# Long-convolution block on one core: the second convolution's windows loaded into 32 partitions, the taps in eight copies

## The reference, cut to what matters

```
q, k, v = u @ Wq.T + bq, u @ Wk.T + bk, u @ Wv.T + bv      # as [batch, channel, position]
k  = causal_conv(k, k_kernel) + k_D * k                    # first convolution, 512 taps a channel
y  = causal_conv(k * v, ssm_kernel) + D * (k * v)          # second convolution, 512 taps a channel
x  = layernorm(u + (y * q) @ Wo.T + bo)
x  = layernorm(x + spikes(relu(x @ W_fc.T)**2 @ W_proj.T))
```

## Time and profile before

| What | Value |
|---|---|
| Median of 3 runs | 1033.93 us (1029.09 to 1037.75) |
| Profiled execution, its own time | 1030.6 us |
| Its span, from the first instruction to the last | 1028.6 us |
| TensorE matmuls busy | 791.5 us, 77% |
| VectorE busy | 712.0 us, 69% |
| ScalarE busy | 521.7 us, 51% |
| Granted TensorE clock over the span | 0.894 |
| Main loop (first to last start of L976) | 78.7 to 479.9 us |

### The profile page before, as it was taken

One profiled execution on the slowest core, in us unless ns is written; L12 is line 12 of the kernel. 1 busy time (PEld: TensorE's weight loads), 2 busy tenths in 40 slices (PEclk: granted clock), 3 DMA queues, 4 the chain that ended last, 5 costly groups with the idle time before them and its releaser, 6 DMA issues.

```text
span 1028.6 us, 27885 instructions
## 1 busy us (share of the span) xinstructions
PE 791.5 (77%) x12032; PEld 648.2 (63%) x12032; DVE 712.0 (69%) x1087; ACT 521.7 (51%) x560; POOL 385.7 (37%) x306
## 2 busy tenths in 40 slices
PE   0186878787768888845499888898888998889983
PEld 0186878787767787845356566665566665666652
DVE  6983555555536665747559877888777878778884
ACT  3475646574645565431445544555445555455551
POOL 0261211121101112200455446655456544565542
PEclk9998989898888989976589998999899989989997
DMA  9898898888767788897000111100111101111001
GB/s 347 287 300 225 181 237 181 227 182 222 177 135 164 157 184 179 184 209 206 20 1 1 42 41 41 41 18 22 41 41 41 36 5 41 41 41 39 2 21 41
DMA packets 39292, 118.35 MB, mean 115 GB/s; under 512 B 3872, under 2 KB 23200, under 8 KB 31008
## 3 DMA queue, kind: packets, MB, share of 16 engines
q1 hardware_dynamic: 37824, 114.71, 43.3%
q10 hardware_dynamic: 1376, 2.23, 0.6%
HBM read 106.69 MB, written 27.01 MB: 130 GB/s over the span
## 4 chain that ended last, share of the span: by engine, by line
issue 25%; DMA 20%; POOL 19%; PE 18%; DVE 14%; ACT 3%; POOLq 0%; SPq 0%; DVEq 0%; ACTq 0%
DMA arena<-kpad_dram 18%; POOL arena L596 10%; PE ps L670 10%; PE ps L648 4%; POOL arena L603 2%; DVE arena L1048 2%; DVE arena L956 2%; POOL arena L585 2%; PE ps L764 2%; DVE arena L1067 2%; POOL arena L590 2%; DVE arena L939 2%; POOL arena L600 1%; PE ps L771 1%; PE ps L728 1%
## 5 line engine op out<-in xcount | busy, mean ns | idle before, releaser
L670 PE MATMUL ps<-arena 128*128 128x64 f16 (+3 forms) x6144 | 190.7, 187 | 78.6 <-DVE arena L956 41.8
L596 POOL TENSOR_TENSOR arena<-arena 128x512 f16<-128x512 f32 x128 | 165.8, 1314 | 198.0 <-ACT arena L484 194.3
L670 PEld LDWEIGHTS ps<-arena 128*128 128x128 f16 x6144 | 185.8, 101 | 81.9 <-issue 80.6
L432 ACT ACTIVATE arena<-arena 64x3584 f16<-64x3584 f16 x60 | 188.7, 3182 | 51.4 <-DVE arena L939 51.3
L648 PE MATMUL ps<-arena 128*128 128x96 f16 x3072 | 150.6, 214 | 74.4 <-DVE arena L901 51.2
L771 PE MATMUL ps<-arena 128*128 128x256 f16 x1536 | 192.7, 287 | 8.7 <-POOL arena L596 6.1
L648 PEld LDWEIGHTS ps<-arena 128*128 128x128 f16 x3072 | 144.9, 103 | 77.1 <-issue 71.1
L771 PEld LDWEIGHTS ps<-arena 128*128 128x128 f16 x1536 | 157.3, 104 | 42.1 <-POOL arena L596 10.8
L764 PE MATMUL ps<-arena 128*128 128x512 f16 x768 | 170.5, 382 | 2.5 <-DVE arena L1074 2.5
L939 DVE TENSOR_TENSOR arena<-arena 64x512 f16<-64x512 f16 x128 | 67.1, 533 | 151.3 <-DMA arena<-kpad_dram 151.2
L555 POOL TENSOR_TENSOR arena<-arena 128x512 f16<-128x512 f32 x32 | 42.7, 1337 | 278.5 <-ACT arena L426 278.5
(11 more groups left out here) (91 smaller groups left out, 702.2 us busy)
## 6 DMA issues: line engine op xcount, KB each, us to landing
arena<-kpad_dram SPq DMA_DIRECT2D x128, 512.0 KB, 6.9
kpad_dram<-ksplit_dram SPq DMA_DIRECT2D x16, 1024.0 KB, 12.1
qy<-in_uT SPq DMA_DIRECT2D x8, 1024.0 KB, 17.5
arena<-in_u SPq DMA_DIRECT2D x16, 512.0 KB, 4.1
out<-arena SPq DMA_DIRECT2D x16, 512.0 KB, 3.0
arena<-in_k SPq DMA_DIRECT2D x2, 512.0 KB, 4.8
ksplit_dram<-arena ACTq DMA_DIRECT2D x2, 512.0 KB, 3.8
arena<-in_wfT SPq DMA_DIRECT2D x1, 1024.0 KB, 13.8
```

Of the source, the lines that this page charges most:

```text
L432: nc.scalar.activation(*shifted(windows_of(0, s, half)), ACT.Copy).then_inc(c1_copied, 1)
L596: nc.gpsimd.tensor_tensor(h16[:, 1, f], h_square[:, f % 4], h16[:, 0, f], ALU.subtract).then_inc(h_lo, 1)
L670: last = nc.tensor.matmul(out[:, ch * COL + delta * B:(ch + 1) * COL], win[:, delta * P:(delta + 1) * P], data(xp, ch)[:, 0:cols], start=( ...
```

## The change

`kpad_dram` holds 8 copies in place of 16. The spreads are made for each group of eight channels in place of each chunk of 32: 64 DMAs with rows of 1 KB (SLICE // 16 = 512 elements) and 8 copies, in place of 16 DMAs with rows of 4 KB and 16 copies. Three groups are spread before the first window load, five more behind the first six window loads, and then one group in each step, eight ahead. The window load of each group waits for its own group's spread.

The second convolution's windows are loaded into partitions 0 to 31 in place of 0 to 63. VectorE masks 32 columns in 32 partitions, copies partitions 0 to 31 to 32 to 63, 32 columns to the right (`shifted_quarter`), and then copies 0 to 63 to 64 to 127 as before. Both widening copies come ahead of both old copies. The first convolution's windows are still loaded into 64 partitions.

```diff
-NCOPY = 16
-SLICE = CH * 2 * L
-EARLY = 4
+NCOPY = 8
+SLICE = G * 2 * L
+AHEAD = 8
+NKP = 2 * AHEAD
...
+        def shifted_quarter(windows):
+            t = windows.rearrange("p c a n -> p (c a) n")
+            return t[QP:HP, :, QP:L], t[0:QP, :, 0:L - QP]
...
-                at, n = piece * SLICE, SLICE // NCOPY
+                at, n = g * SLICE, SLICE // 16
-                    sp.dma_start(dst, src.unsqueeze(1).to_broadcast([NCOPY, NCOPY, n])).then_inc(kpad_out[piece], 16)
+                    sp.dma_start(dst, src.unsqueeze(1).to_broadcast([16, NCOPY, n])).then_inc(kpad_out[g % NKP], 16)
...
-                sp.dma_start(windows[0:HP].rearrange("p c a n -> p (c a n)"),
-                             bass.AP(first.tensor, first.offset, [[ROWS - HP // NCOPY, NCOPY], [-1, HP // NCOPY], [1, row]])
+                parts = QP if conv else HP
+                sp.dma_start(windows[0:parts].rearrange("p c a n -> p (c a n)"),
+                             bass.AP(first.tensor, first.offset,
+                                     [[ROWS - parts // NCOPY, NCOPY], [-1, parts // NCOPY], [1, row]])
                              ).then_inc(t_in[slot], 16)
...
-            spread(0)
+            for g in range(3):
+                spread(g)
             sp.wait_ge(kpad_head, 16)
-            sp.wait_ge(kpad_out[0], 32)
...
-            for piece in range(1, EARLY):
-                spread(piece)
+            for g in range(3, AHEAD):
+                spread(g)
...
-                if s % GPC == 0 and s // GPC + EARLY < NC:
-                    spread(s // GPC + EARLY)
+                if s + AHEAD < NG:
+                    spread(s + AHEAD)
...
                 for half in range(2):
                     dve.wait_ge(c2_masked, 2 * g + half + 1)
+                    nc.vector.tensor_copy(*shifted_quarter(windows_of(1, s, half, final(g)))).then_inc(c2_widened, 1)
+                for half in range(2):
+                    dve.wait_ge(c2_widened, 2 * g + half + 1)
                     nc.vector.tensor_copy(*shifted(windows_of(1, s, half, final(g)))).then_inc(c2_copied, 1)
```

More of the change, by code:

```diff
@@ L27 @@
 HP = P // 2
+QP = P // 4
 ROWS = P + D * 2 * L
-NCOPY = 16
-SLICE = CH * 2 * L
-EARLY = 4
+NCOPY = 8
+SLICE = G * 2 * L
+AHEAD = 8
+NKP = 2 * AHEAD
 NU = 8
@@ L198, in build @@
             sem(n) for n in ("kpad_zero", "kpad_hi", "kpad_lo", "kpad_head", "ksplit_out", "w16_out"))
-        kpad_out = [sem(f"kpad_out{n}") for n in range(NC)]
+        kpad_out = [sem(f"kpad_out{n}") for n in range(NKP)]
         t_in = [sem(f"t_in{n}") for n in range(8)]
@@ L204, in build @@
             sem(n) for n in ("t_zero", "c1_masked", "c2_masked", "c1_copied", "c2_copied"))
-        c1_copied_dve, c1_half, c2_half = (sem(n) for n in ("c1_copied_dve", "c1_half", "c2_half"))
+        c1_copied_dve, c1_half, c2_half, c2_widened = (
+            sem(n) for n in ("c1_copied_dve", "c1_half", "c2_half", "c2_widened"))
         ld_wcur = [sem(f"ld_wcur{r}") for r in range(2)]
@@ L283, in _, with spread @@
                              uT.rearrange("(t p) n -> p t n", p=P)[:, :, n * UP:(n + 1) * UP]).then_inc(ld_u[n], 16)
-            def spread(piece):
-                at, n = piece * SLICE, SLICE // NCOPY
+            def spread(g):
+                at, n = g * SLICE, SLICE // 16
                 for conv in range(2):
@@ L296, in load_windows @@
                 first = kpad_dram[conv, 0, P + (2 * g + half) * row:]
-                if g % GPC == 0 and conv == 0 and half == 0:
-                    sp.wait_ge(kpad_out[g // GPC], 32)
+                if conv == 0 and half == 0:
+                    sp.wait_ge(kpad_out[g % NKP], 32 * (g // NKP + 1))
                 second_place = conv == 1 and g >= NG - GPC and g % 2 == 0
@@ L839, in _ @@
             nc.vector.memset(T[HP:P].rearrange("p k c a n -> p (k c a) n")[:, :, 0:HP], 0.0).then_inc(t_zero, 1)
+            nc.vector.memset(T[QP:HP, 4:6].rearrange("p k c a n -> p (k c a) n")[:, :, 0:QP], 0.0).then_inc(t_zero, 1)
             link(nc.vector.memset(part_max[:, :], 0.0))
@@ L937, in mask @@
                     dve.wait_ge(t_in[4 + half], 16 * (g + 1))
-                tri = windows_of(conv, s, half, final(g))[0:HP].rearrange("p c a n -> p (c a) n")[:, :, 0:HP]
-                nc.vector.tensor_tensor(tri, tri, causal[0:HP, 0:HP].unsqueeze(1).to_broadcast([HP, 2 * HG, HP]),
+                n = QP if conv else HP
+                tri = windows_of(conv, s, half, final(g))[0:n].rearrange("p c a n -> p (c a) n")[:, :, 0:n]
+                nc.vector.tensor_tensor(tri, tri, causal[0:n, 0:n].unsqueeze(1).to_broadcast([n, 2 * HG, n]),
                                         ALU.mult).then_inc((c1_masked, c2_masked)[conv], 1)
@@ L955, in windows2 @@
                     dve.wait_ge(c2_masked, 2 * g + half + 1)
+                    nc.vector.tensor_copy(*shifted_quarter(windows_of(1, s, half, final(g)))).then_inc(c2_widened, 1)
+                for half in range(2):
+                    dve.wait_ge(c2_widened, 2 * g + half + 1)
                     nc.vector.tensor_copy(*shifted(windows_of(1, s, half, final(g)))).then_inc(c2_copied, 1)
             dve.wait_ge(id_done, 2)
-            dve.wait_ge(t_zero, 1)
+            dve.wait_ge(t_zero, 2)
             for quarter in range(GPC):
@@ L1009, in _ @@
                                      ).then_inc(t_zero, 1)
-                    dve.wait_ge(t_zero, 2)
+                    nc.vector.memset(T2[QP:HP].rearrange("p k c a n -> p (k c a) n")[:, :, 0:QP], 0.0
+                                     ).then_inc(t_zero, 1)
+                    dve.wait_ge(t_zero, 4)
                 if s == PAIR - 2:
```

## The result

| | Kernel before | Changed kernel |
|---|---|---|
| Median | 1034.65 us (1029.09 to 1037.75, 4 runs) | 1059.1 us (1053.16 to 1062.83, 4 runs) |
| Ratio to before | | 1.0237, 95% interval 1.0168 to 1.0306 |
| Profiled execution | 1030.6 us, span 1028.6 | 1062.83 us, span 1061.1 |
| Main loop, first to last start of `times_v` | 401.2 us | 434.8 us |

The change makes the kernel slower by 24.5 us. The profiled executions lie 32 us apart, because the one of before is quicker than its median and the one of after slower; what follows reads places and kinds of waits from the traces, and sizes from medians.

A forecast was written before the change was run, and what follows sets the result against it. A loop through late window loads, VectorE's copies and conv2 was taken to bound the kernel. Main-loop steps of 14.0 us (29) and 17.5 (two) gave 441 us for 401, +40, so 1074 us; range 1008 to 1100.

The forecast's parts named there:

- Eight engines for window loads: Main loop: window loads on eight engines instead of keeping their rate take the forecast from 1012 to 1074 us.
- Eight copies put the loads on eight engines: Window loads: the source pattern's outermost count, now eight, cuts each transfer into eight shares on eight engines.
- A first-convolution load takes 4.8 us: Main loop: transfer into 64 partitions at 13.7 GB/s for each of eight engines, between bounds of 2.4 and 4.8 us.
- rival 1: Window loads keep 220 GB/s on 16 or eight engines; step stays 11.1 us, total 1012; chance 0.27 together with Rival 4.
- The widening costs 2.2 us behind the last landing: VectorE in the main loop: two widening copies of 1.16 us each delay conv2 by some 2.2 us every step.
- The half loads pay exactly for it: Main loop: at unchanged load rate, shorter second-convolution loads offset the widening, leaving the step at 11.1 us.
- The equation T = (6.0 + 2.4 + transfers + tail) / 2: Main-loop step: 6.0 us to the first load's issue, 2.4 fixed, transfers, work behind last landing; 11.1 before, 13.5 after.
- The bursts cost 20.3 us: Main loop before: the four steps behind spread bursts cost 20.3 us more than plain ones; the change removes this.
- Stalls of TensorE would be half hidden: Main loop: TensorE's stalls cost 0.9 us a step; about half is hidden by 2.4 us more slack, giving 14.0.
- Rival 2: Main loop: engines drift apart, a load takes about 3.2 us; -4 us, about 1030, no difference; chance 0.13.
- Rival 3: Main loop: instruction fetches share the eight full engines, 1 to 1.5 us more a step, about 1109; within the 0.60 case.
- Rival 4: Main loop: VectorE's 9.9 us of work becomes the limit, adding 0.3 us a step, 1020; chance 0.27 together with rival 1.

The follow-up runs named there:

- e3: Kernel before with only the spreads changed to eight channels each step; 16 copies, all loads into 64 partitions, no widening: 1022.04 us, ratio 0.9897.
- e1: Changed kernel with 16 copies in place of eight, all else of the change kept: 1005.5 us, ratio 0.972.
- e9: e1 with its 16 stored copies, but the window loads' source pattern names only eight of them: 1059.82 us, ratio 1.0217.
- e10: e1 with its 16 stored copies, but the window loads' source pattern names only four of them: 1167.8 us, ratio 1.1261.
- e4: Kernel before with eight copies in place of 16 as the only change, all window loads into 64 partitions: 1122.45 us, ratio 1.0853.
- e2: Changed kernel, eight copies, with each first-convolution load into 64 partitions issued as two loads of 32: 1013.59 us, ratio 0.9809.
- e5: e3 with the two widening copies added, rewriting what the loads had already put there: 1052.72 us, ratio 1.0144.
- e6: e1 without the two widening copies, leaving a quarter of each second-convolution tile out of the computation: 983.53 us, ratio 0.9495.

## Why the prediction was right, point by point

The forecast was slower, 1074 us, with 1050 to 1108 for its case; 1059.1 is in it, by the mechanism that it named. The size is less good: 24.5 us in place of 40. By medians the change comes apart like this:

| Term | Forecast | Measured | From |
|---|---|---|---|
| Fine spreads in place of bursts | -22 (1012 - 1034) | -12.8 | e3 against before |
| Half loads and widening together | 0 | -16.5 | e1 against e3 |
| Eight engines for window loads | +62 (1074 - 1012) | +53.6 | changed kernel against e1 |
| Sum | +40 | +24.3 | |

The second and third terms came out 16.5 and 8.4 us below the forecast, the first 9.2 above. That the total lies only 15.7 us off is partly luck.

*Eight copies put the loads on eight engines.* Right. e9 shows that the outermost count of the pattern does it, as the Trainium skill has it (DMA: Bandwidth & Descriptors, "Why a DMA increments its semaphore by 16 and not by 1"); a window load's semaphore has eight raises at its end in the changed kernel, four in e10 and 16 in e1, and the DMA shares of 0.47 in the changed kernel and 0.51 in e4 are eight of 16 engines.

*A first-convolution load takes 4.8 us.* Nearly right: 4.5, by the landings. It is no constant, since e4's loads of the same shape took 3.9 with the engines full. A half load took 1.2 where the forecast had 1.3. The reason that was given, engines crowding into a part of the partitions, fits e2 and not e10, and stays unproven. With other rows for each engine (e2) the time comes within 8 us of sixteen engines, which is rival 1 on eight engines.

*The widening costs 2.2 us behind the last landing.* Right. From landing to matmuls the chain shows 3.8 us (214.78 to 218.60), before 1.7 (210.64 to 212.35), and e5 cost 30.7 us, 32 by the equation.

*The half loads pay exactly for it.* Here the sum failed. The equation T = (6.0 + 2.4 + transfers + tail) / 2 gave 1.2 us a step for them, 29 x 1.2 = 35; measured were 38.5 and 47.2. The equation counts a step without stalls. The transfers also stood in the way of TensorE's instructions and of the spreads, which it leaves out; that this is where the extra 4 to 12 us are is argued, not shown.

*The bursts cost 20.3 us.* Mis-sized. I counted the four steps behind bursts against plain ones; finer spreads alone brought 12.8 (e3).

*Stalls of TensorE would be half hidden.* More than half: its waits for nothing shown fell from 57.1 to 20.6 us.

*The rest of the layer is untouched.* Right, 1.5 us in the profiled executions.

*What would show it.* The DMA share, 129 GB/s (125 forecast) and the widening copies at 1.15 us came as written. So, nearly, did the loads: a first-convolution load with nothing ahead of it landed 6.7 to 7.5 us after its issue (ten of them, median 7.2), where 7 to 9 was forecast and 5 would have refuted it. The steps came only on average: their mean is 14.0 us and the median 13.5, but five of the 31 lasted 16.4 to 18.4 (the first, fifth, 13th, 15th and 17th), where such lengths were forecast at the two loop jumps alone, and only the 17th is one. Why the others stay long was not looked into. VectorE's wait for DMA was to grow beyond 149.9 us and was 138.7: it spends the time on copies, and TensorE does the waiting.

Rival 1 without its condition is e1, 1005.5 where it said 1012. Rival 2, a drift to 3.2 us a load, didn't come in the changed kernel (4.5 us), though e4 and e10 show rows quicker than 0.6 us once the queues are full. Rival 3, instruction fetches behind full engines, didn't come: TensorE's waits for nothing shown fell. Rival 4, VectorE as the limit, didn't come either: it was busy for 266 of the 412 us between 78 and 490 us.

## What to carry to other kernels

Look at how a load's pattern is cut before you count its bytes: an outermost count of 8 put a load on eight engines, and a fifth fewer bytes moved (93.2 MB in place of 118.4) came with a kernel 2.4% slower, while the same edit with a count of 16 made it 2.8% faster. Read a DMA share of 0.5 twice, since half of the engines may be full. Where a single buffer closes a loop through a load, write the loop down as one equation: each microsecond behind the landing costs about half a microsecond a step. Here that held within 5% with full loads (30.7 us against 32, e5), and less well with half loads (22.0, e1 against e6), where the expectation had TensorE bind once the widening was out.

## What was not expected of the hardware

How a load is cut decides as much as how many engines carry it. The same eight engines with the same bytes took 0.48 us for a row of 8 KB on average with loads into 64 and 32 partitions, and 0.37 us with loads into 32 alone (1059.1 against 1013.59 us). Most rows took from 0.31 us to twice that: 56% of them 0.60 to 0.66 us in the kernel before, 84% of them 0.30 to 0.33 in e2. Four engines cost less than in proportion: 85% of e10's rows took 0.30 to 0.33 us, and the time was 1167.8 us.
